# Near pixels row by row instead of column by column: what TensorE, ScalarE and VectorE read

## The reference

```python
# layer 0: projections over the last axis, a product of rows, a gate
a = h @ Wa + ba;  b = h @ Wb + bb;  g = sigmoid(h @ Wg + bg)      # h = _gn(x)
x = x + (g * einsum('bijk,bikl->bijl', a, b)) @ Wo + bo
# layer 1: deformable 3x3 convolution
z = relu(_gn(x))
offset = conv3x3(z, w_off) + b_off                    # 18 channels: (dy, dx) for each of 9 taps
samp[tap] = bilinear sample of z at (row + ky - 1 + dy, column + kx - 1 + dx), zero outside
x = x + einsum('bckhw,ock->bohw', samp, w_def)
```

## Time and profile before

| | |
|---|---|
| median of three executions | 1642.09 us (1631.22 to 1646.17) |
| the profiled execution, device time | 1645.54 us |
| its span, first to last instruction | 1643.7 us |
| mean granted TensorE clock | 0.986 of full speed |
| PE busy | 1543.9 us, 94% |
| VectorE (DVE) busy | 1111.5 us, 68% |
| ScalarE (ACT) busy | 1052.1 us, 64% |
| GpSimd (POOL) busy | 934.0 us, 57% |
| stage 1 | to about 330 us |
| fill of stage 2 (no samples yet) | about 330 to 380 us |
| bands at full rate | to about 1570 us |

### The profile page before, as it was taken

The page is one execution under the profiler, slowest core; times in us unless marked ns, Lnnn a source line. Parts: engine busy times, 40 slices in busy tenths (PEclk is TensorE's granted clock), DMA queues, the critical chain, the costliest instruction groups (busy, mean ns, idle before and its releaser), DMA issues.

```text
span 1643.7 us, 28193 instructions
## 1 busy us (share of the span) xinstructions
PE 1543.9 (94%) x9875; PEld 1129.6 (69%) x9876; DVE 1111.5 (68%) x1910; ACT 1052.1 (64%) x1500; POOL 934.0 (57%) x734
## 2 busy tenths in 40 slices
PE   4999999937999999999999999999999999999997
PEld 3777787715776667776666676766777677767775
DVE  5988888745666666666666666666666666666653
ACT  2555555527676767767667666666777777666662
POOL 2555555716755555655665656566566566656562
PEclk9999999958999999999999999999999999999999
DMA  4343344246767777777776777777767777777672
GB/s 138 107 119 106 118 118 118 75 166 241 262 260 247 253 240 268 252 253 246 247 251 243 242 252 255 246 249 272 261 237 256 254 256 268 261 243 247 242 238 67
DMA packets 145701, 356.56 MB, mean 217 GB/s; under 512 B 10709, under 2 KB 77808, under 8 KB 145584
## 3 DMA queue, kind: packets, MB, share of 16 engines
q1 hardware_dynamic: 130864, 327.90, 59.1%
q10 hardware_dynamic: 14720, 27.14, 4.7%
HBM read 292.14 MB, written 62.85 MB: 216 GB/s over the span
## 4 chain that ended last, share of the span: by engine, by line
PE 61%; issue 12%; POOL 8%; DVE 8%; DMA 6%; ACT 2%; SPq 0%; ACTq 0%; POOLq 0%; DVEq 0%
PE bank L759 24%; PE pair L731 17%; PE pair L805 7%; DMA hx_all<-hat_x 6%; POOL samples_hi L1496 4%; PE bank L777 4%; DVE offs_lo L1276 3%; PE pair L777 3%; POOL weights L1541 2%; DVE offs_hi L1273 2%; PE pair L742 2%; PE pair L744 2%; ACT samples_hi L985 1%; POOL rstd L1470 1%; POOL samples_lo L1483 1%
## 5 line engine op out<-in xcount | busy, mean ns | idle before, releaser
L1541 POOL TENSOR_TENSOR weights<-hy_all,hx_all 126x512 f32<-126x512 f32 x576 | 756.6, 1343 | 522.0 <-DMA hx_all<-hat_x 381.6
L1300 DVE SCALAR_TENSOR_TENSOR samples_lo<-bank,samples_hi 128x432 f16<-128x432 f32 (+1 forms) x704 | 403.4, 591 | 364.7 <-ACT samples_hi L985 351.5
L759 PE MATMUL bank<-weights,zT 126*128 126x216 f32 (+1 forms) x2816 | 583.0, 344 | 2.7 <-POOL weights L1541 2.3
L759 PEld LDWEIGHTS bank<-weights,zT 126*128 126x128 f32 x2816 | 490.2, 190 | 44.0 <-issue 29.2
L985 ACT ACTIVATE samples_hi<-bank 128x432 f16<-128x432 f32 (+1 forms) x704 | 362.4, 519 | 226.3 <-PE bank L759 216.2
L731 PE MATMUL pair<-samples_hi,w_hi 128*128 128x512 f16 x576 | 218.9, 380 | 1.2 <-DVE y L1334 1.2
L731 PE MATMUL pair<-samples_lo,w_hi 128*128 128x512 f16 x576 | 217.7, 378 | 0.0
L731 PE MATMUL pair<-samples_hi,w_lo 128*128 128x512 f16 x576 | 217.6, 378 | 0.0
L994 ACT COPY zT<-pair 126x512 f32<-126x512 f32 x192 | 112.5, 586 | 112.2 <-PE pair L777 108.0
L927 ACT ACTIVATE z<-raw,norm_band 128x2772 f32<-128x2772 f32 (+3 forms) x80 | 180.0, 2270 | 0.0
L1483 POOL TENSOR_TENSOR samples_lo<-samples_hi,samples_lo 128x512 f16<-128x512 f32 x64 | 74.2, 1159 | 131.1 <-ACT samples_lo L888 131.0
(11 more groups left out here) (138 smaller groups left out, 1944.8 us busy)
## 6 DMA issues: line engine op xcount, KB each, us to landing
hy_all<-hat_y SPq DMA_DIRECT2D x192, 648.0 KB
hx_all<-hat_x SPq DMA_DIRECT2D x192, 648.0 KB
raw<-x_pad SPq DMA_DIRECT2D x68, 272.0 KB, 11.2
x_pad<-hy_all SPq DMA_DIRECT2D x64, 272.0 KB, 3.3
weights<-in_x SPq DMA_DIRECT2D x64, 256.0 KB, 2.9
out<-y SPq DMA_DIRECT2D x32, 512.0 KB, 10.6
hat_y<-hats ACTq DMA_DIRECT2D x64, 252.0 KB
hat_x<-hats ACTq DMA_DIRECT2D x64, 162.0 KB
```

What stands on the lines that cost most here:

```text
L759: mm = nc.tensor.matmul(sampled_pair(b)[:, :, at:at + BR * cols], zT[0:WPIX, w, :], weights[0:WPIX, u, :, w * WC * BR:(w * WC + cols) * BR ...
L1300: nc.vector.scalar_tensor_tensor(out=samples_lo[:, u, :, c0:c1], in0=sampled_pair(b)[:, :, 0:c1 - c0], scalar=1.0, in1=samples_hi[:, u, :, ...
L1541: nc.gpsimd.tensor_tensor(weights[0:WPIX, u, k, :], hy_all[0:WPIX, k, :], hx_all[0:WPIX, k, :], ALU.mult).then_inc(weights_ready, 1)
```

## The change

Near pixels and their two float16 parts get the layout `[channel, row, column]`. ScalarE reads rows of `raw` and writes rows. TensorE's window is taken from that layout with its two free dimensions swapped, so that it still delivers 512 pixels ordered by column, and by row within a column: the innermost step is one row of 66 float16 elements (132 bytes), where it was one element (2 bytes), and the step from a column to the next is one element (2 bytes), where it was 10 elements (20 bytes). Number, order, sizes and semaphores of all instructions are unchanged, and so is everything behind `B_OFF`.

```diff
         z_near = (abg_space[:, 0:(UW + 2) * (BR + 2)]
-                  .rearrange("p (w r) -> p w r", w=UW + 2))
-        z_hi, z_lo = (sb(n, [P, UW + 2, BR + 2], F16) for n in ("z_hi", "z_lo"))
+                  .rearrange("p (r w) -> p r w", w=UW + 2))
+        z_hi, z_lo = (sb(n, [P, BR + 2, UW + 2], F16) for n in ("z_hi", "z_lo"))
@@ convolve_offset_parts
                         bank[B_OFF][at:at + width, :].rearrange("p (w r) -> p w r", r=BR),
-                        woff[:, k, 0:width], pixels[:, kx:kx + UW, ky:ky + BR],
+                        woff[:, k, 0:width], pixels[:, ky:ky + BR, kx:kx + UW].rearrange("p r w -> p w r"),
                         start=(i < 2), stop=(i + 4 >= len(products)), tile_position=(0, at))
@@ cast_z
                     done = nc.scalar.activation(
-                        z_near[:, :, r0:r1],
-                        raw[:, src:src + r1 - r0, left:left + UW + 2].rearrange("p r w -> p w r"),
+                        z_near[:, r0:r1, :], raw[:, src:src + r1 - r0, left:left + UW + 2],
                         ACT.Relu,
```

## The result

The changed kernel takes 1968.45 us (median of six, 1965.06 to 1971.76) against 1640.76 us for the kernel before on the same chip (median of six): ratio 1.1982, 95% interval 1.1939 to 1.2025 (the quotient of the two medians, 1.1997, lies in it). Some executions of a kernel take over 1.5% longer than its fastest; the ratios in this document leave those out. The forecast was 1965 us. All that the change lost lies in TensorE's 18 matmuls.

What follows compares the result with a forecast made beforehand. PE was taken to bound the kernel. Sixty bands at 5.2 us more (313 us), 14 us in the fill, less 3, made a span of 1968 us, adjusted to a forecast of 1965 us; range 1735 to 2090 us.

Steps and rivals of the forecast that it cites:

- ScalarE's part: L950 falls from 1606 to 948 ns, 42 us of busy time, almost all hidden; 2.6 us gained in the fill.
- The wave: L805's matmuls run in eight waves a band; each goes from 0.216 us to 868 ns, 5.2 us more a band.
- two bare steps: Each distant element of TensorE's read in L805 costs 2 x 0.848 ns, 1.70 ns, without ScalarE's 2.4 ns per column.
- equal byte rates and the loss of a pair of neighbours: PE and ScalarE draw four bytes in 0.85 ns, a float16 pair; a step of 132 bytes leaves no pair.
- The sum: Sixty bands add 313 us, four fill bands at low clock 14, ScalarE gives back 2.6: span 1968 us.
- the wait at L742 I leave as it is: PE's wait for the split offsets, nearly all of 18.1 us in 1100 us, stays: what it waits for begins behind L805.
- What was to stay as it was: VectorE's L1310 and ScalarE's L938 and L961 keep their durations.
- The halving: Rival: L805's wave takes 0.432 to 0.490 us, in all 1742 to 1772 us; chance 0.30.
- Full pace: Rival: PE reads distant float16 in L805 at 0.216 us a wave, only ScalarE changes, 1625 to 1640 us; chance 0.11.
- Interference: Rival: two or four streams in L805 compete, 2080 us, or about 2500 if all run alone; chance 0.15 with the clock.
- a sign that its reason is wrong: If `z_hi` and `z_lo` waves in L805 differ by much, one time for a distant element, whoever reads, is wrong.
- The clock: Rival: slow streaming drops the granted clock, 110 us if a tenth of 17 us a band halves; chance 0.15 with interference.

Runs made afterwards that it cites:

- repeat5: Kernel before with five further passes of the nine `z_hi` matmuls in each band, adjacent reads, overwritten by the last pass: 1978.52 us, ratio 1.2029.
- evict: Changed kernel, but TensorE reads rows of 64 adjacent pixels and ScalarE's eviction puts offsets in column order: 1643.01 us, ratio 0.9959 to the kernel before.
- solo: Changed kernel with eight of nine `z_hi` matmuls on the left half of the array, so they run one after another: 2135.35 us (one run).

## Why the prediction was right

**The bound.** PE's sequence sets the band, before and after; `repeat5` shows it by itself.

**ScalarE's part.** 948 ns were taken, 930 measured. Its 42 us were costed at nothing but 2.6 us in the fill; `evict` agrees, with at most 0.8% for all of it.

**The wave.** The value taken, 868 ns, came from two bare steps of ScalarE for each distant element. Measured: 0.88 us for one stream alone, 0.90 for two, 0.96 for four. The right mechanism, a line has its own time whoever reads it, is shown by the steps of 8 and 16 bytes on both engines: 1.71 ns a line for TensorE and 1.86 for ScalarE at 16 bytes. That the price was two bare steps, 1.70 ns, and not the 1.93 of ScalarE's own row, no row had shown; that this choice met the single stream (0.88 us against 0.868) so closely is luck. The prediction also says that four float32 sampling matmuls in 1.00 us give the pace of 0.183 us; they give (1.00 - 0.35) / 3 = 0.217, and only the rows of eight and twelve give 0.183. The argument that led to the price was partly wrong: equal byte rates and the loss of a pair of neighbours have nothing to do with it, since a step of 4 bytes breaks all pairs and costs 0.23 us. For a step of a row that makes no difference to the sum; for a step of 4 bytes the argument would have given double the measured time.

**The sum.** 1968 us of span was forecast and 1968.0 measured. That it fits to the microsecond is luck: two terms were off in opposite directions. The band grew by 5.64 us, not 5.2. Of the 0.43 us more, 0.28 are the three waves of `z_lo` (0.96 us a wave; four streams do not keep the pace of one) and 0.15 the five of `z_hi` (0.90). And "the wait at L742 I leave as it is" was wrong: it ended, because VectorE's split no longer meets GpSimd's multiplications. The mean period was 19.70 us before and 24.87 after, 5.17 more for 5.64 of work; 0.47 us over some 60 bands is 28 us that the longer band gave back. The view of waits names 18.1 us of them from 500 to 1600 us; where the others lay is not itemised. The bands at the lower clock are three, not four: in the kernel before, the fourth convolution, at 388.96 us, already has the `z_hi` part of 1.25 us. They cost 3 x (7.8 - 3.75) = 12 us where 14 were forecast for four, and 61 x 5.64 = 344 us stand in place of 313: 1644 + 344 + 12 - 28 - 3 = 1969 us.

**What was to stay as it was.** L938 and the eviction of the offsets kept their durations (747 and 747, 767 and 778 ns). VectorE's L1310 did not: 1173 became 1487 ns, because it now always meets GpSimd. PE waited for it nowhere between 500 and 1600 us, so the error cost the sum nothing.

**The rivals.** The halving fell: 0.42 us a wave is what distant writes to PSUM cost, not distant reads of SBUF. The Trainium skill, page Advanced Engine Details and Errata, section SBUF Cachelines, asks for two hits in a line; ScalarE's rows agree (two float32 elements to a line 870 ns, one 1416), but for TensorE in float16 two pixels to a line still cost more than double the time (0.49 against 0.22 us), and only about three to a line were free. Full pace fell with the first timeline. Interference is there as a remainder, 0.06 to 0.18 us a wave of four by the averages of the table. The prediction named a sign that its reason is wrong, `z_hi` and `z_lo` waves that differ by much: they differ by 0.06 us on average, and full waves by 11% (0.92 and 1.02 us). The clock did fall in a slow stream (0.83 in `solo`) but took no time there; in the changed kernel it was 1.00 from 400 to 1880 us.

## What to carry to other kernels

Count how many elements of a moving operand share 16 bytes along its innermost step. One such line costs a stream about 1.7 ns, in which TensorE at full clock takes four float16 elements and ScalarE two float32 ones; with clearly fewer to a line (here two for TensorE and one for ScalarE) the instruction slows about in proportion, however short the jump. If an order has to be changed on the way, the eviction from PSUM by ScalarE does it for nothing, TensorE's write does it at half pace, and TensorE's read at a quarter. When the engine that bounds the loop gets longer, look at the small waits of the old schedule: all of them can vanish, as here, because other engines' instructions move apart, and then they are to be subtracted. If VectorE's durations of one line spread widely, look at whether GpSimd runs beside the long ones.

## What the runs showed of the hardware that was not expected

- A step of 4 bytes in float16 is almost free for TensorE (0.23 us a wave), one of 8 bytes more than doubles the time (0.49).
- A stream limited by its reads costs the same at the lower clock: 4.68 us for the `z_hi` part at a granted clock of 0.50, 4.66 at 1.00. And the granted clock can fall while PE is busy all the time (0.83 over one stretch of `solo`, 0.50 within it), in a stretch of such a single stream.
- Full waves of four streams of float16 reads start 1.17 us apart at a row distance of 128 bytes, 1.02 at 132 bytes and 0.88 at 16 bytes. What they compete for stays open.
- Five passes over the same `z_hi` matmuls need 0.226 us a wave where L731 needs 0.216; reading rows of 64 pixels instead of columns of eight brings L805's `z_hi` part from 1.25 to 1.21 us.
- VectorE's subtraction of 512 float32 elements takes 691 to 693 ns whenever no GpSimd instruction is beside it, and 1460 ns on average with one; its eviction of samples from PSUM takes 588 and 592 ns. That is why L1309 got longer (1173 to 1487 ns) while L1272 and L1275 got shorter.
